# Node scores on VectorE instead of TensorE, and node-row scatters behind a gate, in the front of a four-layer graph kernel

## What is computed

```python
x = _layernorm(x + _L0_gnn_ref(x, edge_index, edge_weight, ...))
x = _layernorm(x + _L1_gnn_ref(x, edge_index, ...))   # PNA: max, min, mean, std over a node's edges
x = _layernorm(x + _L2_gnn_ref(x, edge_index, ...))   # attention and a feed-forward layer
x = _layernorm(x + _L3_gnn_ref(x, edge_weight, ...))  # messages, maximum, a feed-forward layer

def _L0_gnn_ref(X, edge_index, edge_weight, p, w_ih, w_hh, b_ih, b_hh, W0):
    score = X @ p / jnp.linalg.norm(p)               # one number for each of the 50000 nodes
    top_vals, top_idx = jax.lax.top_k(score, c)      # c = 128
    X_tilde = X[top_idx] * jnp.tanh(top_vals)[:, None]
    W = _gru_step(X_tilde, W0, w_ih, w_hh, b_ih, b_hh)   # the 128 x 128 weight of this layer
    XW = X @ W
    ...
    deg = jnp.zeros((n,), XW.dtype).at[dst_sl].add(w_sl)
    dinv = jnp.where(deg > 0, jax.lax.rsqrt(deg), 0.0)
    norm = dinv[src_sl] * w_sl * dinv[dst_sl]
    return jnp.zeros_like(XW).at[dst_sl].add(norm[:, None] * XW[src_sl])
```

## Time and profile before

| | us |
|---|---|
| median of 3 runs | 3558.3 (3554.54 to 3558.34) |
| the profiled execution, first to last instruction | 3856.9 |
| of this the front, until the dense block's first instruction | 498.4 |
| its middle, until the first instructions of `message_edges` | 2748 |
| `message_edges` | 610.5 |

### The profile page before, as it was taken

The page is one execution under the profiler, slowest core; times in us unless marked ns, Lnnn a source line. Parts: engine busy times, 40 slices in busy tenths (PEclk is TensorE's granted clock), DMA queues, the critical chain, the costliest instruction groups (busy, mean ns, idle before and its releaser), DMA issues. The chain is left out here.

```text
span 3856.9 us, 54369 instructions
## 1 busy us (share of the span) xinstructions
PE 3033.4 (79%) x11490; PEld 2023.8 (52%) x11490; DVE 2725.5 (71%) x6900; ACT 2299.0 (60%) x5259; POOL 2523.9 (65%) x2721
## 2 busy tenths in 40 slices
PE   3124149999999998899979999979999996777676
PEld 2012035555555555777759999955555553343333
DVE  3005749999999998777769989969999994222222
ACT  2003039999999999777623333439999994232332
POOL 5750069999999998777534444436666763666665
PEclk7557569999999999899989999989999997777777
DMA  5012025555555554444323343322322321222221
GB/s 190 1 36 90 1 76 171 171 168 169 171 164 175 164 176 141 113 123 119 109 86 112 114 112 110 109 81 72 88 83 84 86 82 44 72 73 72 72 68 46
DMA packets 262118, 404.65 MB, mean 105 GB/s; under 512 B 61938, under 2 KB 104135, under 8 KB 262033
## 3 DMA queue, kind: packets, MB, share of 16 engines
q1 hardware_dynamic: 204920, 304.18, 24.6%
q0 software_dynamic: 44032, 73.90, 8.4%
q10 hardware_dynamic: 13081, 25.69, 2.0%
HBM read 213.15 MB, written 194.37 MB: 106 GB/s over the span
## 5 line engine op out<-in xcount | busy, mean ns | idle before, releaser
L256 POOL TENSOR_TENSOR dn_rstd<-dn_var,w_minus_half 128x4 f32<-128x4 f32 x294 | 292.6, 1002 | 16.7 <-DVE dn_var L241 16.5
L1603 POOL DMA_INDIRECT m_src<-table_x,e_src_first x196 | 191.1, 975 | 127.5 <-issue 52.1
L1603 POOL DMA_INDIRECT p_src<-table_x,e_src x196 | 213.1, 1087 | 93.0 <-issue 53.6
L2491 POOL DMA_INDIRECT out_rows<-m_x,e_out_first x196 | 197.6, 1008 | 94.0 <-issue 65.8
L648 POOL DMA_INDIRECT scratch_node_row<-o_own,e_out x196 | 192.0, 979 | 90.7 <-issue 62.4
L1643 POOL DMA_INDIRECT g_own<-in_x,e_dst x196 | 223.9, 1142 | 36.9 <-issue 36.9
L2576 DVE TENSOR_TENSOR m_y<-m_bout,m_own 128x512 f32<-128x512 f32 x49 | 33.9, 692 | 294.3 <-DMA a_typ<-in_type_row 166.3
L1603 POOL DMA_INDIRECT a_src<-table_x,e_src x196 | 200.9, 1025 | 47.6 <-issue 37.5
L1634 POOL DMA_INDIRECT g_src<-scratch_wide,e_src x196 | 192.0, 980 | 58.8 <-issue 46.0
L1409 PE MATMUL n_banks<-w_gru_both,d_xT 128*128 128x256 f32 x784 | 223.6, 430 | 8.6 <-ACT d_xT L1446 8.6
L1409 PEld LDWEIGHTS n_banks<-w_gru_both,d_xT 128*128 128x128 f32 x784 | 192.9, 327 | 71.3 <-ACT d_xT L1446 68.6
(11 more groups left out here) (486 smaller groups left out, 9952.8 us busy)
## 6 DMA issues: line engine op xcount, KB each, us to landing
table_x<-d_x SPq DMA_DIRECT2D x294, 256.0 KB, 2.0
g_src<-in_x_wide SPq DMA_DIRECT2D x97, 262.0 KB
scratch_wide<-g_src SPq DMA_DIRECT2D x97, 262.0 KB
out_rows<-d_x SPq DMA_DIRECT2D x97, 256.0 KB
s_x<-in_x ACTq DMA_DIRECT2D x31, 768.0 KB
table_x<-d_xT SPq DMA_DIRECT2D x49, 256.0 KB
scratch_post<-d_x SPq DMA_DIRECT2D x49, 256.0 KB, 2.0
p_rc<-scratch_rcount SPq DMA_DIRECT2D x49, 256.0 KB
```

The source lines that it names most:

```text
L256: pool.tensor_tensor(self.rstd[s][:], self.var[s][:], minus_half[:], ALU.pow).then_inc(self.rooted[s], 1)
L1603: pool.indirect_dma_start(out=self.rows[s][:, t * P:(t + 1) * P], out_offset=None, in_=self.table, in_offset=bass.IndirectOffsetOnAxis(ap= ...
L2491: pool.indirect_dma_start(out=D["out"], out_offset=bass.IndirectOffsetOnAxis(ap=Ed.out_first[:, at:at + 1], axis=0), in_=x4[s][:, t * P:(t ...
```

## The change

The scores leave PE and ACT. x is loaded 400 nodes to a partition: 125 partitions, 25 chunks of 16 nodes for each of them (2048 numbers a partition, 1 MB), six buffers, the first nine loads issued by ACT ahead of its square root and each later one when a buffer is free. DVE multiplies a chunk by p in place and sums each node's 128 products, so that `score` is 125 rows of 400. The folding's DVE work is cut into pieces, and the chunks are put between them. The folding's last two DVE pieces (`vector_last`, `vector_rows`) move behind the first and the second level of the top 128. PE keeps only the small products. POOL's first scatter waits on `last_made`, the end of PE's `tensor_last` (`turned`), and `EARLY` is 150 in place of 176, so that 150, 8 and 38 scatters stand where 176, 8 and 12 stood.

```diff
-        self.EARLY, self.MIDDLE = 176, 8
+        self.EARLY, self.MIDDLE = 150, 8
...
+    def turned(eng):
+        eng.wait_ge(last_made, 1)
...
     def load(act, j):
...
+        if j >= BUFS:
+            act.wait_ge(summed, j - BUFS + 1)
+        src = bass.AP(tensor=A["x"].tensor, offset=j * CHUNK * P, ap=[[PER_LANE * P, LANES], [1, CHUNK * P]])
+        act.dma_start(x[j % BUFS][0:LANES, :], src).then_inc(loaded[j % BUFS], 16)
...
+    def vector(dve, j):
+
+        rows = x[j % BUFS][0:LANES, :].rearrange("p (r f) -> p r f", f=P)
+        dve.wait_ge(loaded[j % BUFS], 16 * (j // BUFS + 1))
+        dve.tensor_tensor(rows, rows, each(p[0:LANES, :], CHUNK), ALU.mult).then_inc(weighed, 1)
+        dve.wait_ge(weighed, j + 1)
+        dve.tensor_reduce(score[0:LANES, j * CHUNK:(j + 1) * CHUNK], rows, AX, ALU.add).then_inc(summed, 1)
...
         numbered(n1i, i1, n1, basef[:, 0:1])
+        fold["vector_last"](dve)
         for n, r in enumerate(ROWS):
             dve.wait_ge(lists_loaded, 16 * (n + 1))
             best(merged[n], vm[n], im[n])
             if n == 0:
                 numbered(fmi[n], im[n], fm[n], basef[0:r, n + 1:n + 2])
+                fold["vector_rows"](dve)
...
             tables["done"](pool)
+            fold["turned"](pool)
             for t in range(plan.EARLY):
                 Own.scatter(pool, D, Ed, plan, t)
             top["gpsimd_find"](pool)
...
             fold["vector"](dve)
+            for b in range(13):
+                if b < plan.CHUNKS - 6:
+                    marks["vector"](dve, 6 + b)
+                fold["vector_block"](dve, b)
+            for k in range(3):
+                fold["vector_sum"](dve, k)
+                for j in (19 + 2 * k, 20 + 2 * k):
+                    if j < plan.CHUNKS:
+                        marks["vector"](dve, j)
+                fold["vector_own"](dve, k)
+            fold["vector_std"](dve)
+            for j in range(25, plan.CHUNKS):
+                marks["vector"](dve, j)
             top["vector"](dve)
```

More of the change, by code:

```diff
@@ new lines, in fold_weights, with then, centre, constant @@
+    steps = [0]
+    def then(dve, ins):
+        ins.then_inc(step, 1)
+        steps[0] += 1
+        dve.wait_ge(step, steps[0])
+    def centre(dve, out, src):
+        mean = sums[0:src.shape[0], :]
+        then(dve, dve.tensor_reduce(mean, src, AX, ALU.add))
+        then(dve, dve.tensor_scalar(mean, mean, -1.0 / P, None, ALU.mult))
+        then(dve, dve.tensor_scalar(out, src, mean, None, ALU.add))
+    def constant(dve, c, r):
+        then(dve, dve.tensor_copy(crow[:, c * P:(c + 1) * P], r))
@@ L518, in vector @@
[L518 to L525, removed]
@@ L528, in vector @@
[L528 to L547, removed]
@@ new lines, in vector @@
+        centre(dve, W.g1c[:], W.g1c[:])
+        then(dve, dve.tensor_scalar(W.w1_ffn[:], raw["w1"][:], cols[:, G1:G1 + 1], None, ALU.mult))
+        then(dve, dve.tensor_tensor(row[:], rows[0:1, R_BE1, :], rows[0:1, R_B2_FFN, :], ALU.add))
+        centre(dve, row[:], row[:])
+        constant(dve, C_FFN, row[:])
+        centre(dve, row[:], rows[0:1, R_B2_MSG, :])
+        constant(dve, C_MSG, row[:])
+        then(dve, dve.tensor_copy(bias_wide[:].rearrange("p (h d) -> p h d", h=HEADS), over(bias8[:], P // HEADS)))
@@ new lines, in vector_own @@
+    def vector_own(dve, k):
+        dve.wait_ge(own_made, k + 1)
+        then(dve, dve.tensor_copy(W.own[:, k, :], bank[2][:, 0:P]))
+        then(dve, dve.tensor_copy(row[:], bank[3][0:1, 0:P]))
+        if k == 0:
+            centre(dve, rows[0:1, R_B_LIN, :], rows[0:1, R_B_LIN, :])
+            then(dve, dve.tensor_tensor(rows[0:1, R_B_LIN, :], rows[0:1, R_B_LIN, :], bank[3][0:1, P:2 * P], ALU.add))
+            then(dve, dve.tensor_tensor(row[:], row[:], rows[0:1, R_B_LIN, :], ALU.add))
+        constant(dve, C_PNA + k, row[:])
@@ L929, in begin @@
-    def begin(act):
-        for j in range(min(BUFS, Q)):
-            load(act, j)
-    pieces = []
-    for q in range(4):
-        count = max(0, min(Q, plan.NF - q * Q))
-        if count:
-            pieces.append((32 * q, count, slice(0, GROUP)))
-        if q * Q <= plan.NF < (q + 1) * Q and plan.NF < plan.NG:
-            last = slice(0, N - plan.NF * GROUP)
-            pieces = [p for p in pieces if p[0] != 32 * q] + [(32 * q, count + 1, last)]
-            if count:
-                pieces.append((32 * q, count, slice(last.stop, GROUP)))
@@ L944, in move @@
-    def move(act):
-        act.wait_ge(cleared, 1)
-        act.wait_ge(scored, Q)
-        for first, count, cols in pieces:
-            act.copy(score[first:first + count, cols], bank_score[first:first + count, cols]).then_inc(moved, 1)
+    def vector(dve, j):
[4 more added lines that the diff above has]
+        dve.tensor_reduce(score[0:LANES, j * CHUNK:(j + 1) * CHUNK], rows, AX, ALU.add).then_inc(summed, 1)
@@ L951, in done, with top_nodes @@
     def done(eng):
-        eng.wait_ge(moved, len(pieces))
-    return dict(sync=sync, vector=vector, vector_window=vector_window, turn=turn, product=product, copy=copy, begin=begin, move=move, done=done)
-def top_nodes(nc, A, D, W, plan, score, scored, weight, bank):
+        eng.wait_ge(summed, CHUNKS)
+    return dict(load=load, sync=sync, vector_begin=vector_begin, vector=vector, done=done, ahead=BUFS)
+def top_nodes(nc, A, D, W, plan, score, scored, fold, weight, bank):
     LEVELS, LISTS = 2, 8
@@ L1238, in _ @@
         def _(act):
-            marks["begin"](act)
-            for j in range(Q):
-                if j == 5:
-                    tables["scalar_root"](act)
-                marks["copy"](act, j)
-            marks["move"](act)
+            first = min(marks["ahead"] + 3, plan.CHUNKS)
+            for j in range(first):
+                marks["load"](act, j)
+            tables["scalar_root"](act)
+            for j in range(first, plan.CHUNKS):
+                marks["load"](act, j)
             tables["scalar"](act)
```

213 lines of the change are left out of this document (94 added, 119 removed).

## The result

| | before | after |
|---|---|---|
| median, us | 3556.4 (3553.6 to 3558.3, 4 runs) | 3755.0 (3752.2 to 3760.7, 4 runs) |
| ratio | | 1.0564, 95% interval 1.0549 to 1.0579 |
| span of the profiled execution | 3856.9 | 3759.0 |

The change makes the kernel 198.5 us slower. The forecast was 122 us and 3680, in a range up to 3705: right in sign, out of the range in size. The medians rise while the spans fall, as the prediction expected. The profiled execution of after took 3760.7 us, 1.7 more than its span; only the profile of before stands apart from its median. A new recording of the kernel before (`before_again`, in the experiments) took 3554.4 us with a span of 3552.7. In what follows after is compared with that one.

A forecast was written before the change was run, and what follows sets the result against it. It took the recorded front as bound by a stall beside POOL's scatters, absent from timed runs. Fetch 89 us later plus dense block 33 later gave 122 us slower, 3558 + 122 = 3680 us, range 3605 to 3705.

The forecast's parts named there:

- The stall: Front, beside POOL's scatters: each PE instruction costs 1.4 us, 203 us in all, taken as absent from timed runs.
- the missing 298.6 us: Profiled span of before minus its median; 203 us in the front and 76 in the last block were to explain 279.
- Rival (a): The stall is in the timed runs too, so the change removes it: 3485 us, faster; chance 0.11.
- rival (c): Part of the stall is real in timed runs; at a share of 0.6 nothing changes, 3558 us; chance 0.02.
- POOL's 176 scatters end at 262, so they don't hold the fetch up: Front of the kernel before: scatters end at 262 us, ahead of DVE's names and the fetch at 269.
- the predicted 269: Timed kernel before without the stall: DVE's names and the index fetch come at 269 us.
- The chunks: DVE's product and sum on x: 4.5 us a chunk, 112 us for 25; upper end 5.1 and 127.
- The gate at 163 us: POOL's first scatter waits for tensor_last: 4 + 112 + 45 = 161, plus 2, so 163 us (155 to 178).
- DVE sets the pace, not the loads: Front after the change: at 292 GB/s x and the rest load in 100 us, less than DVE's work.
- 150 scatters and the fetch behind them: After the gate: 150 x 1.30 = 195 us on POOL, fetch at 358 us, 89 us later than before.
- rival (b): Scatters are quicker without recording, below 0.90 us each, so DVE's names set the fetch: +52, 3610 us; chance 0.05.
- The dense block's head: 38 scatters ahead of the first root in place of 12: 26 x 1.285 = 33 us later, uncovered.

The follow-up runs named there:

- gate_only: The kernel before with POOL's first scatter waiting for the end of tensor_last, EARLY still 176, scores on PE: 3605.1 against 3553.7 us, ratio 1.0150.
- rest38_only: The kernel before with EARLY 150 in place of 176, so 38 scatters at the dense block's head: 3576.7 against 3553.7 us, ratio 1.0073.
- fill_waits: The kernel before with EARLY 172 and MIDDLE 12, a scatter behind each index fetch ahead of its wait: 3551.9 against 3555.2 us, ratio 0.9986.
- split_112: The changed kernel with each chunk of x loaded by two transfers, partitions 0 to 111 and 112 to 124: 3700.9 us against 3553.7 before, ratio 1.0425.
- weights_first: split_112 with ACT letting the folding's weights land before the fifth chunk of x: 3689.4 us against 3552.6 before, ratio 1.0389.
- no_gate_176: weights_first without the gate and with EARLY 176: 3599.8 us against 3552.6 before, ratio 1.0133.

## Why the sign was right and the size wrong

**The stall is not in the timed kernel: right, and decisive.** The prediction found the missing 298.6 us in the two stretches in which POOL scatters, and concluded that the timed kernel fetches at 269 us. It fetches at 265.9, and the last block's scans come every 10.09 us. Rival (a) fell with the timed runs and again with gate_only, and rival (c) with it. What was too much is the reason given, "something that recording does": two more recordings of the same program show nothing of it. The rule of the Trainium skill that was quoted beside it (page "NOTIFIC — the notification-queue block", section 7.1) is neither shown nor refuted by these runs.

**"POOL's 176 scatters end at 262, so they don't hold the fetch up": wrong by 8 us.** DVE's names are ready at 257.9, and POOL's queue sets the fetch at 265.9. Two errors nearly cancel here: the first MAX8 came at 123.9 and not 135, so the names were 11 us earlier than the predicted 269, and POOL's scatters ended some 4 us later than 262. That the fetch of 269 was off by 3 us only is in part luck. The step moved the sum by these 3 us, but it is why rest38_only cost 23 and not 33, and why fill_waits gains.

**The chunks: right.** 4.5 us predicted, 4.53 measured; the product takes 2.29 us, and so does the sum.

**The gate at 163 us: this is the step that failed.** It opened at 234.1. "DVE sets the pace, not the loads" took 292 GB/s from the earlier trace rows, a rate of other transfers, for x in a new shape. The new transfer has 125 rows, runs on 5 engines and brings 131 GB/s, so 25 chunks need 25 x 7.7 = 193 us and not 100. The sum took the 125 partitions for the size of DVE's work and not for the shape of a transfer. Of the 71 us by which the gate came late, two transfers in place of one take 51 back (183.1, split_112), the order of the weights 13 more (170.2, weights_first), and 7 stay.

**The wait for the folding's weights: left out.** The sum had "a first wait of some 4 us" as its only wait. In after DVE waited 35.7 us for the last weight, for which the sum had nothing. These 35.7 us don't stand behind the 193 of x's stream but mostly beside them: x's queue filled the six buffers meanwhile and paused only from 111 to 121 us, so I estimate from the trace that it held the stream up by some 10 us. The wait goes with slow issues of the weights' loads. SP's timeline in after shows one that takes 7.35 us, and 1.78 in rest38_only:

```profile
52.91 7.35 SPq L456 DMA_DIRECT2D w_w1b<-in_L_W  x1
```

**150 scatters and the fetch behind them: right.** (431.9 - 234.1)/150 = 1.32 us each with what stands between, predicted 1.30. So rival (b), quicker scatters outside a recording, fell: after's profiled execution took as long as the others. The names came 136.1 us behind the first MAX8, predicted 136.5, and had 63 us of cover, predicted 60.

**The dense block's head: right.** 33 predicted, 31.6 in after against before_again, 33.4 from the block's start in rest38_only. Uncovered, as said.

With the gate at 234.1 in place of 163 the prediction's own sum is 122 + 71 = 193, and with the fetch of before 3 us earlier 196; 198.5 were measured. The runs put it together in another way: 47 for the scores on DVE with good supply (no_gate_176), 90 for the gate and the split of the scatters (3689.4 - 3599.8), 10 for the weights' order and 51 for the five engines (with the part of the weights' wait that goes with them), each by the distances from before, 198.5 in all.

## What to carry to other kernels

When a transfer gets a new shape, its rate is a new unknown: take the number of rows, ask how many engines can share them evenly, and work out the time of the stream before saying that an engine sets the pace. Where a profile's span and the timed runs disagree, find the place of the difference and then record the same program again. A gate in front of a long queue of fixed cost moves the whole queue: here a gate 51 us sooner made the kernel 51 to 54 us faster (split_112), and one 13 us sooner 10 to 12 (weights_first).

## What the runs showed of the hardware

- A transfer issued by ACT whose slowest dimension is 125 rows ran on 5 DMA engines at 131 GB/s, one of 124 on 4 at 104, about 26 GB/s for each engine in both. 112 + 13 rows fed DVE, at 4.5 us of work a chunk, with no wait after the first.
- x's loads, issued by ACT, delayed SP's issues, more so on five engines, but also on 16. SP's 29 weight loads were issued by 30.3 us in rest38_only, where ACT loads x in the old shape, by 61.4 in split_112 and by 79.5 in after, where ACT's first nine issues took 43.6 us (in weights_first the median issue of a part of a chunk took 0.42). Held ahead of most of x in weights_first, they were issued by 34.6. What makes an issue slow was not tested.
- One recording was 300 us longer than the kernel's timed runs, in two stretches with scatters; in the first of them each PE instruction took 1.4 us. In the eleven others the span is 1.7 to 1.8 us under the time of the same execution.
